# Two-part float32r scores for the destinations of a graph layer, and a later change of lag

## The reference

```python
h = einsum('ni,hio->hno', x, W)
attn_src = einsum('hno,hod->hn', h, a_src)
attn_dst = einsum('hno,hod->hn', h, a_dst)
e = attn_src[:, src_idx] + attn_dst[:, dst_idx]
e = where(e >= 0, e, 0.2 * e) * edge_weight
e_exp = exp(e - max(e))
denom = segment_sum(e_exp, dst_idx)
out = segment_sum(h[:, src_idx] * e_exp / (denom[:, dst_idx] + 1e-10), dst_idx)
```

## Time and profile before

| what | value |
|---|---|
| median of three runs | 2397.0 us (2392.29 to 2398.76) |
| profiled execution | 2396.2 us, its span 2394.1 us |
| TensorE, clock granted on average | 0.88 of full speed |
| PE busy | 1902.2 us, 79% of the span |
| PE weight loads busy | 1623.5 us, 68% |
| VectorE busy | 1426.5 us, 60% |
| ScalarE busy | 1211.2 us, 51% |
| GpSimd busy | 1522.9 us, 64% |

### The profile page before, as it was taken

How to read it: one execution, slowest core, us unless ns; L and a number is a source line. 1 busy time by engine, 2 the same in 40 slices (tenths; PEclk the granted TensorE clock), 3 DMA queues, 4 the chain that set the end, 5 groups by cost and what they waited for, 6 DMA issues and landing times. The chain is left out here.

```text
span 2394.1 us, 38204 instructions
## 1 busy us (share of the span) xinstructions
PE 1902.2 (79%) x12132; PEld 1623.5 (68%) x12132; DVE 1426.5 (60%) x4037; ACT 1211.2 (51%) x2298; POOL 1522.9 (64%) x1253
## 2 busy tenths in 40 slices
PE   7799999989999999999999999954245555455560
PEld 7688888878888888888888888843133444333350
DVE  6556666656666666666666666653165455454475
ACT  2477777757777777777777777734000000000012
POOL 0427777777787777777777777734655565555513
PEclk9899999999999999999999999977566676766685
DMA  7798877777777777777777887674344444444423
GB/s 247 253 237 198 179 169 163 153 152 157 163 163 161 161 165 160 164 163 162 163 162 169 175 177 174 134 198 122 97 110 121 120 131 118 119 114 122 114 80 110
DMA packets 239706, 370.92 MB, mean 155 GB/s; under 512 B 33255, under 2 KB 172481, under 8 KB 239495
## 3 DMA queue, kind: packets, MB, share of 16 engines
q0 software_dynamic: 104688, 191.38, 40.5%
q1 hardware_dynamic: 134807, 177.00, 25.0%
HBM read 260.28 MB, written 107.97 MB: 154 GB/s over the span
## 5 line engine op out<-in xcount | busy, mean ns | idle before, releaser
L1549 POOL DMA_INDIRECT accA<-ystage,to_a x391 | 639.3, 1635 | 204.7 <-issue 105.7
L1555 POOL DMA_INDIRECT GA<-TA,src_c x391 | 436.5, 1116 | 246.0 <-issue 108.5
L1606 POOL DMA_INDIRECT Hg<-HT,src_c x391 | 376.2, 962 | 266.9 <-DVE xb L1118 152.0
L644 DVE TENSOR_TENSOR h2l<-h2f,h2h 128x512 fp32r<-128x512 f32 (+1 forms) x294 | 203.2, 691 | 307.3 <-ACT h2h L1997 159.9
L1681 PE MATMUL bank<-h1h,W1h 128*128 128x512 f32 x882 | 355.1, 403 | 12.9 <-DVE h1l L644 12.9
L1682 PE MATMUL bank<-h1l,W1h 128*128 128x512 f32 x882 | 349.0, 396 | 0.0
L1683 PE MATMUL bank<-h1h,W1l 128*128 128x512 f32 x882 | 348.8, 395 | 0.0
L2034 ACT ACTIVATE h1f<-bank 128x512 f32<-128x512 f32 (+1 forms) x392 | 220.7, 591 | 243.0 <-PE bank L1736 196.8
L1926 PE MATMUL bank<-xb,in_window 128*128 128x260 f32 (+1 forms) x782 | 277.3, 501 | 62.5 <-issue 60.7
L2177 ACT ACTIVATE drop<-neg_m 128x1 f32<-128x1 f32 x49 | 14.4, 295 | 548.9 <-DVE neg_m L1113 376.5
L1926 PEld LDWEIGHTS bank<-xb,in_window 128*128 128x128 f32 (+1 forms) x782 | 187.9, 252 | 112.7 <-issue 82.2
(11 more groups left out here) (252 smaller groups left out, 4498.3 us busy)
## 6 DMA issues: line engine op xcount, KB each, us to landing
ef<-in_eT SPq DMA_DIRECT2D x97, 256.0 KB
bcast_i<-in_src_row SPq DMA_DIRECT2D x97, 256.0 KB
TW<-TB SPq DMA_DIRECT2D x116, 203.0 KB
HB<-hist SPq DMA_DIRECT2D x98, 130.0 KB
rel<-RL SPq DMA_DIRECT2D x97, 128.0 KB
rem<-RD SPq DMA_DIRECT2D x48, 256.0 KB
TB<-stB SPq DMA_DIRECT2D x24, 406.0 KB
accA<-zeros SPq DMA_DIRECT2D x4, 2193.0 KB, 15.6
```

Of the source, the lines that this page charges most:

```text
L644: return dve.tensor_tensor(o, full, hi.bitcast(f32), ALU.subtract)
L1549: return pool.indirect_dma_start(out=table, out_offset=bass.IndirectOffsetOnAxis(ap=rows, axis=0), in_=sums, in_offset=None, compute_op=AL ...
L1555: pool.indirect_dma_start(out=GA[0:n, b % (GAR * BLOCKS_PER_GROUP), :].bitcast(f32), out_offset=None, in_=TA, in_offset=bass.IndirectOffse ...
L1606: pool.indirect_dma_start(out=Hg[0:n, slot, :], out_offset=None, in_=HT, in_offset=bass.IndirectOffsetOnAxis(ap=src_c[0:n, b:b + 1], axis= ...
```

## The change

- In layer 2, ad_p has two parts instead of three, in float32r, the two next to each other for each group (8 columns). hot is float32r instead of bf16, at the same number of elements.
- `destination_scores` has one product for each block: 128 columns of hot as weights, 8 columns of ad_p as moving data. It leaves the two parts' scores side by side in PSUM.
- `edge_scores` adds first the one part to the gathered source scores, then, after a wait, the other part. There is one more step of s_sc for each pair (SCS = 4), and `destination_scores` waits for the second addition of the pair before.
- `window_scores` has two operations less (a rounding copy and a subtraction through `lo`, a helper that other places of the kernel use for the low part of a split).
- `chosen` is no array of its own any more but lies in the slots 2 to 11 of Hg; `ad_rest` is gone.
- SLOW_START is 91 instead of 20: the groups up to 90 are added three steps behind, those from 91 two, and the step with the additions of two groups is step 93 (groups 90 and 91).

```diff
--- before.py
+++ after.py
@@ -9,7 +9,7 @@
 TABLES = 2
 Y_RING = 24
 WHOLE_RUNS = 80
-SLOW_START = 20
+SLOW_START = 91
 SPILLED = 32
 SPILL_RING = 4
 TILE_STEPS = 9
@@ -314,8 +314,7 @@
         ADC = 14
         picked = sb("picked", [P, ADC, HEADS, NT], f32, sc)
         ad_w = sb("ad_w", [P, NG, HEADS], f32, sc)
-        ad_rest = sb("ad_rest", [P, ADC, HEADS], f32, sc)
-        ad_p = sb("ad_p", [P, 3, NG, HEADS], bf16, sc)
+        ad_p = sb("ad_p", [P, NG, 2, HEADS], f32r, sc)
         score = sb("score", [P, NB, HEADS], f32, sc)
         top_c = sb("top_c", [P, NQ], f32, sc)
         neg_m = sb("neg_m", [P, NQ + 1], f32, sc)
@@ -323,7 +322,6 @@
         drop_k = sb("drop_k", [P, NQ], f32, sc)
         last_g = sb("last_g", [P, NT, NG], bf16, sc)
         factor = sb("factor", [P, NG], f32, sc)
-        chosen = sb("chosen", [P, NT, NG], f32, sc)
         scale = sb("scale", [P, NT], f32, sc)
 
         Wc = sb("Wc", [P, DK, OUT + 2 * HEADS], f32, sc)
@@ -336,8 +334,10 @@
 
         HGR = 12
         Hg = sb("Hg", [P, HGR * BLOCKS_PER_GROUP, BW], f32, sc)
+        chosen = Hg[:, 2 * BLOCKS_PER_GROUP:HGR * BLOCKS_PER_GROUP, :].rearrange("p b d -> p (b d)")[:, 0:NT * NG]\
+            .rearrange("p (t g) -> p t g", g=NG)
         rem = sb("rem", [P, 2, 2 * GE], bf16, s2)
-        hot = sb("hot", [P, 2, 2 * GE], bf16, s2)
+        hot = sb("hot", [P, 2, 2 * GE], f32r, s2)
         XBR = 4
         xb = sb("xb", [P, XBR * BLOCKS_PER_GROUP, BW], f32, s2)
         in_window = sb("in_window", [P, XBR * BLOCKS_PER_GROUP, P], f32, s2)
@@ -397,7 +397,7 @@
 
 
         iota_p, node_p = bank[2][:, 0:P], bank[2][:, P:P + NT * HEADS].rearrange("p (t h) -> p t h", h=HEADS)
-        QH = 2 * BLOCKS_PER_GROUP * HEADS
+        QH, ADP, SCS = 2 * BLOCKS_PER_GROUP * HEADS, 2 * HEADS, 4
 
         def weight_p(q):
             return bank[3 + q % 2][:, 0:QH].rearrange("p (k h) -> p k h", h=HEADS)
@@ -1042,10 +1042,8 @@
                                         node_p.rearrange("p t h -> p h t").unsqueeze(1).to_broadcast([P, ADC, HEADS, NT]),
                                         in_tile[:, v, :].unsqueeze(2).to_broadcast([P, ADC, HEADS, NT]), ALU.mult))
                 const(dve.tensor_reduce(ad_w[:, v, :], picked[:, :, :, :], AX.X, ALU.add))
-                const(dve.tensor_copy(ad_p[:, 0, v, :], ad_w[:, v, :]))
-                const(dve.tensor_tensor(ad_rest[:, :, :], ad_w[:, v, :], ad_p[:, 0, v, :], ALU.subtract))
-                const(dve.tensor_copy(ad_p[:, 1, v, :], ad_rest[:, :, :]))
-                dve.tensor_tensor(ad_p[:, 2, v, :], ad_rest[:, :, :], ad_p[:, 1, v, :], ALU.subtract).then_inc(s_adw, 1)
+                const(dve.tensor_copy(ad_p[:, v, 0, :], ad_w[:, v, :]))
+                lo(ad_p[:, v, 1, :], ad_w[:, v, :], ad_p[:, v, 0, :]).then_inc(s_adw, 1)
 
             def one_hot(q):
 
@@ -1074,26 +1072,30 @@
                 dve.wait_ge(s_hg[2 * q % HGR], group_arrivals(HGR, 2 * q))
                 dve.wait_ge(s_hg[(2 * q + 1) % HGR], group_arrivals(HGR, 2 * q + 1))
                 dve.wait_ge(s_ad, q + 1)
-                for run in runs:
-                    n, b, k = rows_of_block(run[0]), run[0], len(run)
-                    j, r = b - blocks[0], b % (HGR * BLOCKS_PER_GROUP)
-                    last = dve.tensor_tensor(
-                        score[0:n, b:b + k, :], Hg[0:n, r:r + k, OUT:BW],
-                        PAD[0:n, j * HEADS:(j + k) * HEADS].rearrange("p (k h) -> p k h", h=HEADS), ALU.add)
-                last.then_inc(s_sc, 1)
-                dve.wait_ge(s_sc, 3 * q + 1)
+                for part in range(ADP // HEADS):
+                    if part:
+                        dve.wait_ge(s_sc, SCS * q + part)
+                    for run in runs:
+                        n, b, k = rows_of_block(run[0]), run[0], len(run)
+                        j, r = b - blocks[0], b % (HGR * BLOCKS_PER_GROUP)
+                        last = dve.tensor_tensor(
+                            score[0:n, b:b + k, :], score[0:n, b:b + k, :] if part else Hg[0:n, r:r + k, OUT:BW],
+                            PAD[0:n, j * ADP:(j + k) * ADP].rearrange("p (k c) -> p k c", c=ADP)[:, :, part * HEADS:(part + 1) * HEADS],
+                            ALU.add)
+                    last.then_inc(s_sc, 1)
+                dve.wait_ge(s_sc, SCS * q + SCS - 2)
                 for run in runs:
                     n, b, k = rows_of_block(run[0]), run[0], len(run)
                     v = score[0:n, b:b + k, :]
                     last = dve.scalar_tensor_tensor(v, v, NEG_SLOPE, v, ALU.mult, ALU.max)
                 last.then_inc(s_sc, 1)
-                dve.wait_ge(s_sc, 3 * q + 2)
+                dve.wait_ge(s_sc, SCS * q + SCS - 1)
                 for run in runs:
                     n, b, k = rows_of_block(run[0]), run[0], len(run)
                     v = score[0:n, b:b + k, :]
                     last = dve.tensor_tensor(v, v, w_c[0:n, b:b + k].unsqueeze(2).to_broadcast([n, k, HEADS]), ALU.mult)
                 last.then_inc(s_sc, 1)
-                dve.wait_ge(s_sc, 3 * q + 3)
+                dve.wait_ge(s_sc, SCS * (q + 1))
                 dve.tensor_reduce(top_c[:, q:q + 1], score[:, blocks[0]:blocks[-1] + 1, :].rearrange("p b h -> p (b h)"),
                                   AX.X, ALU.max).then_inc(s_topc, 1)
                 dve.wait_ge(s_topc, 2 * q + 1)
@@ -1899,12 +1901,11 @@
                 pe.wait_ge(s_hot, q + 1)
                 pe.wait_ge(s_adw, 2 * q // ADC + 1)
                 if q >= 1:
-                    pe.wait_ge(s_sc, 3 * (q - 1) + 1)
+                    pe.wait_ge(s_sc, SCS * (q - 1) + ADP // HEADS)
                 for j, b in enumerate(blocks_of_window_pair(q)):
                     n = rows_of_block(b)
-                    for part in range(3):
-                        last = pe.matmul(PAD[0:n, j * HEADS:(j + 1) * HEADS], hot[:, q % 2, j * P:j * P + n],
-                                         ad_p[:, part, b // BLOCKS_PER_GROUP, :], start=part == 0, stop=part == 2)
+                    last = pe.matmul(PAD[0:n, j * ADP:(j + 1) * ADP], hot[:, q % 2, j * P:j * P + n],
+                                     ad_p[:, b // BLOCKS_PER_GROUP, :, :].rearrange("p i h -> p (i h)"), start=True, stop=True)
                 last.then_inc(s_ad, 1)
 
             def spread_maxima(q):
```

## The result

The changed kernel takes 2368.7 us (median of four runs, 2366.2 to 2374.83); the kernel before took 2397.41 beside it. The ratio is 0.9875, its 95% interval 0.9846 to 0.9903. The profiled execution has a span of 2366.5 us against 2394.1, 27.6 us less. The forecast was 2300: the sign is right and the value lies in the range, but the gain is under a third of what was said (28 of 97 us).

What follows compares the result with a forecast made beforehand. In layer 2, while gathers run, PE was taken to lag by a cost per instruction, holding VectorE and then GpSimd. 2396.2 - 91 (stall) + 4 (VectorE) - 12 (lag) = 2297, said as 2300 us; range 2235 to 2390.

Steps and rivals of the forecast that it cites:

- code that comes late over the DMA engines: Layer 2: inferred that PE runs late while gathers run, perhaps for its code, at a cost for each instruction.
- Stall: 13.8 us, 0.082 us for each of 168 instructions: Layer 2, cycle of two pairs: stall falls to 8.6 us with 104 instructions, gaining 3.8 us a cycle, 91 us in all.
- The count of cycles: Layer 2 gathers: 24 pauses in 641.4 us taken as cycles of two pairs, 26.7 us each; gain multiplied by 24.
- VectorE's 0.71 us a pair: Layer 2: one-hot +0.48 us and second score addition 0.23 us on each pair; +4 us in the tail.
- The lag: First layer: SLOW_START 91 moves the step with two groups' additions from 22 to 93; -12 us, ends -20 and 0.
- The 17 us of step 22: First layer: five groups behind the change of lag take 90.9 us and should take 74.0; 17 us lost.
- Only PE's steps 95 to 97 remain behind it: First layer, behind step 93: only the chain of last additions suffers, so 4 to 5 us come back.
- 0 (all returns): First layer: end of the range for the change of lag, where the whole gain is given back; 0 us.
- B: Layer 2: stall hangs on the burst alone and falls below the gathers, GpSimd never waits; 2236 to 2241 us, chance 0.19.
- F: Layer 2: float32r products count twice, 136 instructions, stall 11.2 us, gain 29 us; 2359 us, chance 0.08.
- E: Late signal unrelated to the number of products, VectorE's new work hidden, only the lag counts; 2384 us, chance 0.11.
- C: Layer 2: stall set by the gathers, 13.8 us a cycle as before, VectorE's 0.71 us on every pair; 2419 us, chance 0.12.

Runs made afterwards that it cites:

- f2: Kernel before with each bf16 product of destination_scores done twice (48 for a pair); slower kind of chip: 2489.0 us, ratio 1.0378.
- f3: Kernel before with three bf16 parts in one product of 12 columns and three additions on VectorE, SLOW_START 20; slower kind: 2365.4 us, ratio 0.9863.
- f1: The changed kernel unedited, run once more on the slower kind of chip: 2374.1 us, ratio 0.9896 to the kernel before.
- f4_hot_tt: Changed kernel with the one-hot written by tensor_tensor instead of tensor_scalar; slower kind: 2353.3 us, ratio 0.9787.
- e1_lag_only: Kernel before with only SLOW_START changed from 20 to 91; faster kind: 2204.0 us, ratio 0.9987.
- e4_lag90: Changed kernel with SLOW_START 90 instead of 91, so no tile is due in the double step; faster kind: 2216.2 us, ratio 1.0036.
- g3_merged_lag21: Kernel before with three bf16 parts in one product of 12 columns and SLOW_START 21; faster kind: 2211.8 us, ratio 1.0006.
- e2_product_only: Changed kernel with SLOW_START back at 20, the product alone; faster kind: 2217.1 us, ratio 1.0050.

## Why the prediction was right or wrong

**What bounds the kernel: right for the slower kind of chip.** The score waits for TensorE's signal, not for rows, and its instructions count: f2 and f3 moved the time by +87 and -36 us; f2 changed nothing else, and f3 only added work to VectorE. The prediction's guess at the reason, code that comes late over the DMA engines, finds no support: no packet of code lands within the long waits. Why the signals come late is open.

**The step that failed** is "Stall: 13.8 us, 0.082 us for each of 168 instructions". As VectorE's idle time the 13.8 us a cycle are right: (640.3 - 301.1) / 24.5 = 13.8. To charge all of it to the instructions was not. The runs give 0.034 to 0.041 us an instruction, half the price, and some 7.5 us a cycle that stay. For 104 instructions the forecast was 8.6 us a cycle, measured were 293.7 / 24.5 = 12.0. What stays is near the 170 / 24.5 = 6.9 us that VectorE idles on the faster kind, waiting for the pace of the gathers. The prediction had the means to see it: by its own rows a cycle of gathers takes 20.0 us, so of 26.7 us at most 6.7 could be lateness.

With the cost of lateness taken against the faster kind (145 us, 0.035 us an instruction), an estimate of the term is 64 x 0.035 x 24.5 = 55 us gained, less 21 of added work on VectorE and 8 of longer gathers: 26 us instead of 91. The stretch lost 24 to 25 (f1) and 19 (the result). That the sum comes out does not prove its parts, and f4_hot_tt, which adds work and gets faster, contradicts the second.

The count of cycles came out by luck: the prediction divided by 24 pauses as if there were one in each two pairs. There are 24.5 cycles, but the pauses are not tied to them; f2_six_parts has 37 pauses in as many cycles.

**VectorE's 0.71 us a pair** was too much: a pair of the tail takes 2288.24 - 2281.41 = 6.83 us (start of L1111 to the next) against 6.43, so 0.4 us. The second addition cost its 0.22 us. The one-hot takes 754 ns, not 970: the nearest row, doubled, was too high a price. The ratio of 2 that the prediction took from the Trainium skill ("VectorE: DVE Perf Modes", section "The perf-mode tier table") doesn't hold for the whole instruction either: 754 to 490 ns is 1.54, and the measurement decides.

```profile
2281.41 0.28 DVE L1111 TENSOR_REDUCE top_g<-bank 128x1 f32<-128x128 f32 x1
...
2288.24 0.28 DVE L1111 TENSOR_REDUCE top_g<-bank 128x1 f32<-128x128 f32 x1
```

**Float32r weights.** The load of L1907 takes 239 ns mean, the product 304, against 99 and 165 in bf16. The Trainium skill ("TensorE: Matmul & The Clock Gate", section "Weight-path perf modes — Fast Weight Load (FWL) and DoubleRow") gives the fast load to 128 weights whose dtype is not FP32, and doesn't name float32r. The trace fits float32r weights going without it; eight products take 1.14 us in the tail against 0.75 for 24. It changed nothing there, as said.

**The lag: -12 was said, about -3 is measured** (e1_lag_only, not told from 0). The 17 us of step 22 were right to the microsecond. "Only PE's steps 95 to 97 remain behind it" failed: the loss falls on the next two groups and is as large there as at step 22. I had priced only the chain of GpSimd's last additions, and not the tile's load behind them, for which VectorE and then TensorE wait 10 us. Moving the double step away from a tile doesn't help (e4_lag90, g3_merged_lag21), so the eight additions are the likely cost; that is argued, not shown. The bound "0 (all returns)" was the right end.

**Not in the forecast at all:** the longer one-hot holds up gathers, 8 us by the two windows. It is small on the slower kind beside the pauses, and the whole effect of the product on the faster one.

**Of the rivals,** none happened as told. B is out by the 115 to 123 us of waits for xb that are left, F by the records; E, "only the lag counts", gave 2384 and is 15 us off; C had its mechanism half right: one half of VectorE's idle time does not go with the instructions. On the faster kind the changed product ends on the slower side, e2_product_only with 1.0050 and e4_lag90, the nearest run to the whole change, with 1.0036, by a mechanism that no rival had. The sign of the forecast holds on the slower kind only.

## What to carry to other kernels

A stall that has been seen at one load has no slope yet: before an engine's idle time is divided by a count, take off what it would idle anyway, here because another engine's gathers set the pace, and ask what would stay at a count of zero. Where a pause starts when a ring is full, what a change moves is in the main how often it comes. And a wait whose releaser the profile can't name may belong to the chip and not to the kernel: here an edit that gains 1.2% on one chip has parts that lose 0.5% on another, and three bf16 parts in one product (f3) keep the gain on the one at no cost on the other (g3, the same layer 2).

## What the runs showed of the hardware

- The same program takes 2397 to 2402 us on one kind of chip and 2206 to 2210 on another. The difference is in layer 2: 391 gathers in 641 us and in 496, and 37 us behind the last of them. On the faster kind GpSimd's pauses for xb are 0.3 us at most. Why TensorE's signals come late on the one is not known.
- On the slower kind the signals often come 1.9 (f2) or 3.0 us (before) after the last gather of a run of gathers has ended, but in the kernel before 17 of 31 late ones, the longest with 33 us among them, come while gathers go on. Whether a stop releases them wasn't seen.
- They are not late for want of code: within the 13 longest waits of the kernel before, no packet of the queue lands that, by its count of packets (19, 29 and 13), carries TensorE's code.
- A gather's descriptor writing that begins while VectorE compares 128x1024 elements mostly ends about 0.8 us after that instruction's end, for tensor_scalar (0.75 us) and for tensor_tensor (1.22 us), where it takes 0.95 us otherwise.
- f4_hot_tt, with 23 us more work on VectorE and longer gathers, is 21 us faster than the changed kernel on the slower kind and 13 us slower than e2_product_only's ratio would give on the faster one (1.0107 against 1.0050). Only the first is odd; I have no cause for it.
